# Five weight loads: from the sync engine's order to one run on ScalarE's DMA queue

## What is computed

```python
x = x + mixer(layernorm(x))
x = x + ffn(layernorm(x))

def mixer(u):
    zxbcdt = u @ W_in.T                      # z0, x0, xBC, dt
    xBC = silu(causal_conv4(xBC) + conv_b)   # per channel, 4 taps
    dt = softplus(dt + dt_bias)
    # state scan over time: h = exp(dt*A)*h + dt*x*B ; y = h.C + D*x
    y = layernorm(y) * ln_gamma + ln_beta
    y = sigmoid(y @ W_gate.T + b_gate) * y
    return concat([silu(z0) * x0, y]) @ W_out.T

def ffn(x):                                  # tern(W): -1, 0 or 1 by mean |W|
    h = gelu(x @ tern(W_fc).T)
    return (layernorm(h) * ln_w + ln_b) @ tern(W_proj).T
```

## Time and profile before

| | us |
|---|---|
| median of 3 runs | 1181.17 |
| lowest, highest | 1180.12, 1182.61 |
| the profiled execution | 1182.05 |
| its span in the profile | 1180.3 |
| PE busy | 1120.7 (95%) |
| DVE busy | 984.8 (83%) |
| ACT busy | 924.6 (78%) |
| POOL busy | 399.1 (34%) |
| DMA queue q1 | 87.67 MB, 34.6% of 16 engines' time |
| granted TensorE clock, mean | 0.983 of full speed |

### The profile page before, as it was taken

One profiled execution on the slowest core, in us unless ns is written; L12 is line 12 of the kernel. 1 busy time (PEld: TensorE's weight loads), 2 busy tenths in 40 slices (PEclk: granted clock), 3 DMA queues, 4 the chain that ended last, 5 costly groups with the idle time before them and its releaser, 6 DMA issues. The chain is left out here.

```text
span 1180.3 us, 23293 instructions
## 1 busy us (share of the span) xinstructions
PE 1120.7 (95%) x8534; PEld 722.1 (61%) x8534; DVE 984.8 (83%) x1958; ACT 924.6 (78%) x1651; POOL 399.1 (34%) x500
## 2 busy tenths in 40 slices
PE   4778999999999999999999999999999999999986
PEld 1354756666575666657565675766657575767663
DVE  5999998989798898879898997898969898676654
ACT  4957578888888797878878888887888878787845
POOL 1122234142612524242442423333244422334422
PEclk9879999999999999999999999999999999999998
DMA  5520213333423424342242523324344331324455
GB/s 185 153 46 1 65 37 74 64 90 64 101 44 68 103 38 100 64 116 42 46 95 46 117 54 73 82 38 107 46 98 88 68 74 29 79 43 94 78 102 108
DMA packets 238978, 89.16 MB, mean 76 GB/s; under 512 B 207760, under 2 KB 235152, under 8 KB 238864
## 3 DMA queue, kind: packets, MB, share of 16 engines
q1 hardware_dynamic: 238864, 87.67, 34.6%
HBM read 24.32 MB, written 8.39 MB: 28 GB/s over the span
## 5 line engine op out<-in xcount | busy, mean ns | idle before, releaser
L359 PE MATMUL bank<-xnT,win 128*128 128x512 f16 (+1 forms) x1248 | 299.0, 385 | 22.0 <-DMA xnT<-hb 20.8
L359 PEld LDWEIGHTS bank<-xnT,win 128*128 128x128 f16 (+1 forms) x1248 | 121.5, 101 | 155.3 <-issue 31.4
L945 DVE SCALAR_TENSOR_TENSOR cv<-bank,cws,cv 128x510 f32<-128x510 f32 (+5 forms) x240 | 178.1, 744 | 7.7 <-ACT bcu L672 0.9
L359 PE MATMUL bank<-yhl,wg 128*128 128x512 f16 x768 | 174.3, 382 | 2.8 <-DVE yhl L1092 2.0
L1212 POOL TENSOR_TENSOR cat<-sz,cat 128x512 f16<-128x512 f32 x64 | 86.6, 1356 | 237.4 <-ACT cat L782 237.4
L587 PE MATMUL bank<-wpj,hT 128*128 128x256 f16 x1024 | 129.1, 282 | 13.7 <-DMA hT<-hb 12.1
L359 PEld LDWEIGHTS bank<-yhl,wg 128*128 128x128 f16 x768 | 73.9, 98 | 92.6 <-issue 6.8
L587 PEld LDWEIGHTS bank<-wpj,hT 128*128 128x128 f16 x1024 | 101.5, 101 | 39.0 <-issue 16.1
L180 ACT ACT_TABLE_LOAD x95 | 121.9, 1283 | 2.4 <-PEq L1386 0.7
L575 PE MATMUL bank<-wfc,x3T 128*128 128x512 f16 x512 | 120.7, 379 | 0.0
L1208 POOL TENSOR_TENSOR caty<-tg,caty 128x512 f16<-128x512 f32 x64 | 81.0, 1275 | 109.5 <-ACT caty L770 109.3
(11 more groups left out here) (145 smaller groups left out, 2109.1 us busy)
## 6 DMA issues: line engine op xcount, KB each, us to landing
x<-in_x SPq DMA_DIRECT2D x32, 512.0 KB, 4.2
out_y<-x SPq DMA_DIRECT2D x15, 512.0 KB, 3.2
crep<-cv SPq DMA_DIRECT2D x128, 32.0 KB, 2.0
hT<-hb SPq DMA_TRANSPOSE x128, 3.1
caty<-in_wg SPq DMA_DIRECT2D x1, 1024.0 KB, 6.8
x<-in_wout SPq DMA_DIRECT2D x1, 1024.0 KB, 6.7
segR<-segL SPq DMA_DIRECT2D x64, 6.0 KB
hT<-in_wfc SPq DMA_DIRECT2D x1, 1024.0 KB, 5.1
```

The costliest lines, as they stand in the source:

```text
L359: m = eng.matmul(b, lhs(p, k), rhs(q, k), start=(n == 0), stop=(n == len(seq) - 1))
L945: op = eng.scalar_tensor_tensor(cs[0:w, j, 3 - k:T], b[0:w, 0:T - 3 + k], cws[0:w, j, k:k + 1], cs[0:w, j, 3 - k:T], ALU.mult, ALU.add)
```

## The change

The five calls of `weights` leave SP. The function moves to ScalarE under the name `weights_load` and the letter `M`, with the same transfers and semaphores; in `ACT_ORDER` five `M0` stand in one run between the last `W0` and the first `c0`. In `SP_ORDER` the five `W0` are taken out, all else keeps its place. Since the transfers are now started by ACT, they go to a DMA queue of their own.

```diff
 ACT_ORDER = (
-    "N0 a0 h0 W0 W0 c0 c0 c0 a1 10 h1 30 c0 c0 z0 z0 s0 40 b0 s0 l0 c1 50 z0 e0 c1 c1 D0 f0 E0 11 c1 E0 c1 F0 F0 "
+    "N0 a0 h0 W0 W0 M0 M0 M0 M0 M0 c0 c0 c0 a1 10 h1 30 c0 c0 z0 z0 s0 40 b0 s0 l0 c1 50 z0 e0 c1 c1 D0 f0 E0 11 "
...
 SP_ORDER = (
-    "h0 h0 W0 K0 K0 h1 h1 W0 c0 60 W0 W0 h2 h2 c1 61 h3 h3 62 r0 c2 X0 X0 W0 h4 r1 h4 63 c3 j0 j0 j0 j0 j0 j0 j0 "
+    "h0 h0 K0 K0 h1 h1 c0 60 h2 h2 c1 61 h3 h3 62 r0 c2 X0 X0 h4 r1 h4 63 c3 j0 j0 j0 j0 j0 j0 j0 j0 p0 X1 h5 X1 "
...
+            def weights_load(i, n):
+                if n == 0:
+                    eng.dma_start(wgs, wg_d.rearrange("(k p) n -> p k n", p=P)).then_inc(ld_wg, 16)
+                elif n == 1:
+                    eng.dma_start(wos, wout_d.rearrange("(k p) n -> p k n", p=P)).then_inc(ld_wout, 16)
+                elif n == 2:
+                    eng.dma_start(wfs.rearrange("p (k n) -> p k n", k=2), wfc_d.rearrange("(k p) n -> p k n", p=P)
+                                  ).then_inc(ld_wfc, 16)
+                elif n == 3:
+                    eng.dma_start(wps.rearrange("p (k n) -> p k n", k=8), wpj_d.rearrange("(k p) n -> p k n", p=P)
+                                  ).then_inc(ld_wpj, 16)
+                else:
+                    eng.dma_start(lnwb[:, :], lnw_d).then_inc(ld_lnw, 16)
+
...
-            STEPS = {"W": weights_in, "N": minus_a, "D": weights_gate, "O": weights_out, "F": weights_abs, "a": norm_x,
+            STEPS = {"M": weights_load, "W": weights_in, "N": minus_a, "D": weights_gate, "O": weights_out, "F": weights_abs, "a": norm_x,
...
-            STEPS = {"K": constants, "W": weights, "h": turn_x, "c": spread_c, "6": rows, "r": residual, "X": turn_x2,
+            STEPS = {"K": constants, "h": turn_x, "c": spread_c, "6": rows, "r": residual, "X": turn_x2,
                      "j": turn_h, "p": store}
```

More of the change, by code:

```diff
@@ L1260, in constants @@
                               ).then_inc(ld_c16, 16)
[L1262 to L1274, removed]
             def turn_x(i, n):
```

## The result

| | before | changed |
|---|---|---|
| median, us | 1181.63 | 1193.03 |
| lowest, highest | 1180.12, 1182.61 | 1192.85, 1194.88 |
| runs | 4 | 4 |
| profiled execution | 1182.05 | 1192.98 |
| its span | 1180.3 | 1190.5 |

The changed kernel is slower: ratio 1.0097, 95% interval 1.0084 to 1.0110, or +11.4 us on the medians. The forecast was +3.7 with a range up to 1191. The direction was right, the size a third of the truth, and the time lies outside the range.

The account below looks back on a forecast made before the run. The prediction took DVE to bound the first 110 us and PE the rest. Between +3.2 for PE and ACT and +4.1 for DVE it took +3.7, giving 1184.9 against a 1181.17 median; range 1179.5 to 1191.

Parts of the forecast that it names:

- What bounds the kernel: Whole kernel: the first 110 us are DVE's, the rest PE's; what PE loses in the opening is never given back.
- Five issues leave SP: SP's issue order: some 2.7 us of issues go, gain on the path 0, at most 0.6 us.
- Five issues come to ACT: ACT between last W0 and first c0: 2.7 us of issues fit in the 4.54 us wait for PE, cost 0.
- The bound from above: ACT's five issues: each as long as a transpose's, 1.36 us, ending at 22.8, 2.3 us too late for c0.
- When they start: ACT's issues: from 12.4 us if the sequencer runs ahead of activations, 16.0 if it waits; 12.4 was taken.
- What the transfers meet: Block 0's transposes: the weights run beside them and delay PE's first matmul by 3.2 us, from 17.65 to 20.9.
- the equal split: DMA engines in the opening: both queues get equal time, so 3.2 us of transposes take 6.4, +3.2.
- rival B: Block 0's transposes: queues alternate one packet each, small packets starve; transposes +9.2, x +10.7, time 1191; chance 0.18.
- The x load: x block 1 behind the transposes: 3.0 instead of 1.5 us, so 4.7 later in all; DVE's first tap +4.5.
- the slack of 0.41 at hb: DVE before hb (30.24): 0.41 us of slack, leaving +4.1 of the first tap's +4.5 delay.
- Constants and second transposes: After x block 1: constants land near 28, hidden; transfers end at 34.0, just clear of second transposes' bytes at 35.
- Earlier weights: Later waits for weights: only proj was waited for, ACT some 0.5 us; PE is not late there, gain 0.

Follow-up runs that it names:

- the gate load alone: Against the kernel before, only the gate load moved to ACT at 12.5 us, the four others left in SP's order: 1184.98 us, ratio 1.0017.
- the runs behind c0: Against the kernel before, loads on ACT behind the first c0: five 1185.82, four 1187.3, three 1182.77, two 1182.98; two, with three more behind the first c1, 1184.56 us.

## Why the prediction was wrong

*What bounds the kernel.* Right in the main. The opening is DVE's and nearly all that it loses stays lost: DVE was 12.1 us late at the first tap and 11.5 us late on block 1, the span is 10.2 us longer, and PE's busy time from 140 to 1100 us is the same within 1.2 us.

*Five issues leave SP: 0.* Right; with two or three loads placed elsewhere the time is unchanged.

*Five issues come to ACT: 2.7 us, hidden.* The size was wrong, the cover held. The five took 0.43, 0.52, 0.69, 1.22 and 5.83 us, 8.7 in all, because the last was held. ACT had nothing to do until 32.28, so it cost nothing here; behind the first c0 the same holding moved the second c0 by 5.4 us. The bound from above, 1.36 us for each, was drawn from the wrong kind of row: no row read from the trace of before showed an issue that is held. What the issue waits for was not tested.

*When they start: 12.4.* Right, 12.54: the sequencer runs ahead of the activations.

*What the transfers meet.* Here is the step that failed: "I take the equal split, as neither side has a row that prefers it." The term was +3.2 and measured +11.75. Two things stood in its place: 1 MB of weights passed before the first transposed packet (17.7), and after that the queues shared by equal counts of packets and not by time. The second was rival B, to which 0.18 was given. B's own price, +9.2 at the transposes and 1191, was short too, as it let the turns begin at 14.1. An estimate from these runs: the gate load alone cost 2.54; behind it 2048 transposed packets let pass 1024 of 1 KB (out), 256 of 4 KB (fc) and 768 of 1 KB (proj), 2.88 MB or 8.3 us at 349 GB/s; together +10.8 of the +11.75. The rest is open. That the collision in block 0 makes the loss is shown by the runs behind c0, in which the first matmul and, with two or three loads, the time are those of before.

The Trainium skill ("DMA: Bandwidth & Descriptors", section Queues, rings and completion order) says that an engine goes round its queues packet by packet, where a packet is typically some 9 to 17 descriptors. Equal counts in this trace agree with going round by packets (570 to 566, 86 to 86); how many pieces go in one turn can't be seen in them. The MB that passes alone is not in that rule; there the measurement decides.

*The x load: another +1.5.* Half of it: x(1) came 12.4 us late, 0.7 more than the first matmul. DVE's first tap was 12.1 late and its first tap on block 1 11.5; of that 0.6, the slack of 0.41 at hb was reckoned.

*Constants and second transposes: hidden, all transfers done at 34.0.* Right: the engines are idle from 34 us, the second pair is issued at 41.61.

*Earlier weights: 0.* Right. ACT's wait for proj is gone, and PE's wait for the sums is 3.3 us instead of 4.3, but its wait for S grew from 1.6 to 2.2 us (the waits of PE from 28 to 122 us):

```profile
PE bank L366 <- ACT h L647: 3.3, 1, 3.3
PE bank L494 <- DVE S L1068: 2.2, 1, 2.2
```

*The range* ended at 1191, B's price, and so held only half of B. With the head start of the gate load, +1.6 by the estimate above, B would stand at about 1192.6.
